# Four of the eight FFN-input passes in fp16 instead of fp32r, in a fused cross-attention and FFN kernel

## The reference

```python
x = x + xattn(layernorm(x), ctx)         # q, k, v, softmax over 256 keys, Wo
x = x + ffn(layernorm(x))
...
def ffn(x):
    h = bitlinear(x, w_fc) + gate * (x @ v.T @ fast_b.T @ u.T)
    r = jnp.maximum(h, 0.0)
    return bitlinear(r * r, w_proj)
def bitlinear(x, w):
    scale = clip(mean(abs(w), axis=1, keepdims=True), 1e-5)
    tern = clip(round(w / scale), -1.0, 1.0)       # -1, 0 or 1
    return x @ (tern * scale).T
```

## Time and profile before

| | us |
|---|---|
| median of the three runs | 782.87 |
| lowest, highest | 781.95, 783.26 |
| profiled execution, span | 782.9 |
| TensorE busy (share) | 769.6 (98%) |
| VectorE busy | 547.3 (70%) |
| ScalarE busy | 368.8 (47%) |
| GpSimd busy | 107.1 (14%) |

### The profile page before, as it was taken

The page is one execution under the profiler, slowest core; times in us unless marked ns, Lnnn a source line. Parts: engine busy times, 40 slices in busy tenths (PEclk is TensorE's granted clock), DMA queues, the critical chain, the costliest instruction groups (busy, mean ns, idle before and its releaser), DMA issues.

```text
span 782.9 us, 10596 instructions
## 1 busy us (share of the span) xinstructions
PE 769.6 (98%) x3767; PEld 639.7 (82%) x3767; DVE 547.3 (70%) x1118; ACT 368.8 (47%) x690; POOL 107.1 (14%) x125
## 2 busy tenths in 40 slices
PE   7999999999999999999999999999999999999997
PEld 4578788888888888888888888888888888888886
DVE  4899776867767687767767786768667686656434
ACT  4899644363434545344533644254442644233332
POOL 3101220200311020110312011210202003000001
PEclk9999999999999999999999999999999999999999
DMA  9644341073214422073214422063212530030101
GB/s 275 245 152 145 54 95 41 1 108 68 81 41 65 66 71 95 1 106 71 80 41 54 69 80 94 2 91 57 109 41 32 80 92 1 1 54 2 53 0 55
DMA packets 180126, 56.20 MB, mean 72 GB/s; under 512 B 167621, under 2 KB 167895, under 8 KB 180073
## 3 DMA queue, kind: packets, MB, share of 16 engines
q1 hardware_dynamic: 149940, 50.79, 26.9%
q10 hardware_dynamic: 30132, 4.73, 3.7%
HBM read 26.92 MB, written 8.39 MB: 45 GB/s over the span
## 4 chain that ended last, share of the span: by engine, by line
PE 95%; SPq 1%; DMA 1%; DVE 1%; issue 0%; ACT 0%; POOL 0%; POOLq 0%; DVEq 0%; ACTq 0%
PE H L1357 30%; PE O L1338 29%; PE G L1220 26%; PE H L1363 4%; PE H L1220 1%; PE H L1204 1%; DMA Wv_s<-in_L_xattn_Wv_dram 1%; PE O L1412 1%; PE G L1304 1%; PE H L1197 1%; PE O L1378 0%; PE G L1248 0%; SPq L518 0%; SPq L556 0%; PE O L1395 0%
## 5 line engine op out<-in xcount | busy, mean ns | idle before, releaser
L1338 PE MATMUL O<-projT,qbuf 128*128 128x512 f32 x992 | 242.1, 390 | 0.0
L1338 PEld LDWEIGHTS O<-projT,qbuf 128*128 128x128 f32 x992 | 185.0, 188 | 38.2
L779 ACT ACTIVATE rbuf<-H,scf 128x512 f32<-128x512 f32 x128 | 87.5, 683 | 125.2 <-DVE qbuf L1116 73.5
L1357 PE MATMUL H<-even_group,fcT 128*128 128x512 f32 x512 | 127.5, 391 | 0.0
L1357 PE MATMUL H<-odd_group,fcT 128*128 128x512 f32 x512 | 127.3, 391 | 0.0
L1112 DVE TENSOR_TENSOR rbuf<-rbuf 128x512 f32<-128x512 f32 x128 | 91.4, 722 | 46.4 <-ACT rbuf L779 46.4
L787 ACT ACTIVATE qbuf<-rbuf 128x512 fp32r<-128x512 f32 x125 | 78.6, 628 | 89.5 <-PE O L1338 62.6
L1116 DVE TENSOR_TENSOR qbuf<-rbuf,qbuf 128x512 fp32r<-128x512 f32 x125 | 85.8, 687 | 37.0 <-ACT qbuf L787 36.2
L1357 PEld LDWEIGHTS H<-odd_group,fcT 128*128 128x128 f32 x512 | 95.3, 188 | 19.3
L1357 PEld LDWEIGHTS H<-even_group,fcT 128*128 128x128 f32 x512 | 95.1, 188 | 19.2
L1220 PE MATMUL G<-Wvo,tT 128*128 128x512 f32 x270 | 64.7, 389 | 0.0
(11 more groups left out here) (194 smaller groups left out, 993.3 us busy)
## 6 DMA issues: line engine op xcount, KB each, us to landing
xb<-in_x_dram SPq DMA_DIRECT2D x8, 1024.0 KB, 5.2
n_blocks<-n_rows SPq DMA_DIRECT2D x112, 64.0 KB, 2.3
ctxb<-in_ctx_dram SPq DMA_DIRECT2D x8, 768.0 KB, 4.4
n_blocks<-ctxb SPq DMA_DIRECT2D x112, 48.0 KB, 2.2
wring<-in_L_ffn_w_fc_dram SPq DMA_DIRECT2D x16, 256.0 KB, 5.8
wring<-in_L_ffn_w_proj_dram SPq DMA_DIRECT2D x16, 256.0 KB, 2.7
out_dram<-x2a SPq DMA_DIRECT2D x8, 512.0 KB, 2.7
x_blocks<-x_rows SPq DMA_DIRECT2D x56, 64.0 KB, 3.5
```

The costliest lines, as they stand in the source:

```text
L779: nc.scalar.activation(rbuf[:, j % 2, :], banks[f"H{j % 2}"][:, :], ACT.Relu, scale=scf[:, j:j + 1]).then_inc(relu_made, 1)
L1338: mm = pe.matmul(banks[f"O{t}"][:, :], qbuf[:, j % 2, h, t * P:(t + 1) * P], projT[:, j, :], start=(j == 0 and h == HI), stop=(j == NFF - ...
L1357: pe.matmul(banks[f"H{j % 2}"][:, :], fcT[:, k, j * P:(j + 1) * P], xnT[:, h, k, :], start=(k == 0 and h == HI), stop=False)
```

## The change

The high half of the FFN input is now an fp16 array of its own (`hi16_of`, laid over a part of the group's array). In `up` four passes multiply it by the ternary weights read as bf16, which is the upper two bytes of each fp32 word (`fc16`, every second 2-byte element); then four passes in fp32r take the low half, which is now the rest over fp16. Before, high and low alternated. `L` keeps fp32r, so GpSimd copies the fp16 halves into fp32r places that are free then (`xhi32`): four new steps `x32:k` in the prologue and in bodies 0 to 6. L waits for all four. In the prologue each of them waits for the last ScalarE copy of x.

```diff
@@ orders of the steps (ACT and DVE of BODY_ORDER; POOL of all three) @@
-        "hi:11 up:12 nc0+ xhi0 up:13 xhi1 xhi2 hi:12 hi:13 up:14 up:15 hi:14 nc1+ nc2+ hi:15 xhi3 nc3+ "
+        "hi:11 up:12 nc0+ xhi0 up:13 xhi1 xhi2 hi:12 hi:13 up:14 up:15 hi:14 xhi3 nc1+ hi:15 nc2+ nc3+ "
-        "residual xs23+ a:0 a:1 a:2 a:3 cs23+ "
+        "residual xs23+ a:0 a:1 a:2 a:3 cs23+ x32:0 x32:1 x32:2 x32:3 "
...
@@ buffers @@
+        hi16_of = [None, under("odd_hi16", [P, KD, TOK], FP16)]
...
+        hi16_of[0] = under("even_hi16", [P, KD, TOK], FP16)
...
+        fc16 = fcT[:, :, :].bitcast(BF16).rearrange("p k (n h) -> p k n h", h=2)[:, :, :, 1]
+
+        def xhi32(g, k):
+
+            return group_of[(g + 1) % 2 if k < 2 else g % 2][:, HI, 2 + k % 2, :]
@@ GpSimd @@
+                    elif st[0] == "x32":
+
+                        k = st[1]
+                        if b < 0:
+                            pool.wait_ge(unit_act, n_act(b, ("x", 3)))
+                            pool.wait_ge(rounded_made, 28)
+                        else:
+                            pool.wait_ge(xhi_made, KD * b + k + 1)
+                        nc.gpsimd.tensor_copy(xhi32(g, k), hi16_of[g % 2][:, k, :]).then_inc(xhi32_made, 1)
@@ ScalarE: x in the prologue, xhi in the bodies @@
-                    nc.scalar.activation(group_of[0][:, HI, :, cols], wide, ACT.Copy).then_inc(unit_act, 1)
+                    nc.scalar.activation(hi16_of[0][:, :, cols], wide, ACT.Copy).then_inc(unit_act, 1)
...
-                        nc.scalar.activation(halves[:, HI, k, :], raw[:, LO, k, :], ACT.Copy).then_inc(xhi_made, 1)
+                        nc.scalar.activation(hi16_of[(b + 1) % 2][:, k, :], raw_of[(b + 1) % 2][:, LO, k, :], ACT.Copy
+                                             ).then_inc(xhi_made, 1)
@@ VectorE: xlo in the bodies (x in the prologue likewise) @@
-                        nc.vector.tensor_tensor(halves[:, LO, k, :], raw[:, LO, k, :], halves[:, HI, k, :],
+                        nc.vector.tensor_tensor(halves[:, LO, k, :], raw[:, LO, k, :], hi16_of[(b + 1) % 2][:, k, :],
                                                 ALU.subtract).then_inc(xlo_made, 1)
@@ TensorE: L @@
+                    highs = [(FB[:, k, :], xhi32(b, k)) for k in range(KD)]
+                    pe.wait_ge(xhi32_made, KD * (b + 1))
                     if b == 0:
                         job_read(pe, JOBS.index(("fb", 0)))
-                        pe.wait_ge(unit_act, n_act(-1, ("x", 3)))
-                        products(bank[:, :], [(FB[:, k, :], xnT[:, HI, k, :]) for k in range(KD)], last=False)
+                        products(bank[:, :], highs, last=False)
                         pe.wait_ge(unit_dve, n_dve(-1, ("x", 3)))
...
                     else:
-                        pe.wait_ge(xhi_made, KD * b)
-                        products(bank[:, :], [(FB[:, k, :], xnT[:, HI, k, :]) for k in range(KD)], last=False)
+                        products(bank[:, :], highs, last=False)
                         pe.wait_ge(xlo_made, KD * b)
@@ TensorE: up @@
                         for k in range(KD):
-                            for h in (HI, LO):
-                                pe.matmul(banks[f"H{j % 2}"][:, :], fcT[:, k, j * P:(j + 1) * P], xnT[:, h, k, :],
-                                          start=(k == 0 and h == HI), stop=False)
+                            pe.matmul(banks[f"H{j % 2}"][:, :], fc16[:, k, j * P:(j + 1) * P], hi16_of[b % 2][:, k, :],
+                                      start=(k == 0), stop=False)
+                        for k in range(KD):
+                            pe.matmul(banks[f"H{j % 2}"][:, :], fcT[:, k, j * P:(j + 1) * P], xnT[:, LO, k, :],
+                                      start=False, stop=False)
```

More of the change, by code:

```diff
@@ L239 @@
     "pool": (
-        "scale:0 tb xs23 scale:1 scale:2 cs23 scale:3 scale:4 scale:5 scale:6 scale:7 B.xs23 a:0 a:1 a:2 a:3 B.cs23 "
+        "scale:0 tb xs23 scale:1 scale:2 cs23 scale:3 scale:4 scale:5 scale:6 scale:7 B.xs23 a:0 a:1 a:2 a:3 x32:0 x32:1 x32:2 x32:3 B.cs23 "
     ).split(),
@@ L366, in mk_xattn_ffn, with under @@
         setup.close()
-        def under(name, shape):
+        def under(name, shape, dt=F32):
             with ExitStack() as below_it:
-                return sb(name, shape, F32, below_it)
+                return sb(name, shape, dt, below_it)
         raw_of = [None, under("odd_halves", [P, 2, KD, TOK])]
+        hi16_of = [None, under("odd_hi16", [P, KD, TOK], FP16)]
         odd = sb("odd_group", [P, 2, KD, TOK], F32R)
@@ L438, in mk_xattn_ffn @@
         xraw_made, xhi_made, xlo_made = sem("xnT_raw_made"), sem("xnT_hi_made"), sem("xnT_lo_made")
+        xhi32_made = sem("xnT_hi_made_for_the_low_rank_passes")
         MOVES = 16 * 16
@@ L809, in steps @@
                         k = int(kind[3])
-                        raw, halves = raw_of[(b + 1) % 2], group_of[(b + 1) % 2]
                         act.wait_ge(xraw_made, KD * b + k + 1)
-                        nc.scalar.activation(halves[:, HI, k, :], raw[:, LO, k, :], ACT.Copy).then_inc(xhi_made, 1)
+                        nc.scalar.activation(hi16_of[(b + 1) % 2][:, k, :], raw_of[(b + 1) % 2][:, LO, k, :], ACT.Copy
+                                             ).then_inc(xhi_made, 1)
                     elif kind == "xmove":
@@ L957, in unit @@
                 if kind == "x":
-                    nc.vector.tensor_tensor(group_of[0][:, LO, :, cols], wide, group_of[0][:, HI, :, cols], ALU.subtract
+                    nc.vector.tensor_tensor(group_of[0][:, LO, :, cols], wide, hi16_of[0][:, :, cols], ALU.subtract
                                             ).then_inc(unit_dve, 1)
```

## The result

| | before | after |
|---|---|---|
| median of 8 runs, us | 782.84 | 786.2 |
| lowest, highest | 781.95, 783.26 | 783.53, 789.52 |
| profiled execution, span | 782.9 | 786.7 |
| TensorE weight loads busy | 639.7 | 588.5 |
| VectorE busy | 547.3 | 557.3 |

After takes 1.0042 times as long as before, interval 1.0023 to 1.0061: 3.4 us slower, where 782.1 us was forecast. A run's time is its span and some 2 us outside it, so the profiled execution of after is the run of 788.88 us, the second slowest of its eight, and that of before, with a span of 782.9 and 1.8 us outside, stands for some 784.7 us and not for the median.

The account below looks back on a forecast made before the run. TensorE's matmul passes times their spacing were taken as the bound. Spacing -5.4, L's wait +3.0, clock +1.6 and bodies 0 gave -0.8 us from 782.9, so 782.1 us; range 779.6 to 785.0, likeliest case's own 780.4 to 783.8.

Parts of the forecast that it names:

- Part 1: TensorE `up` steps: 512 passes going from fp32r to fp16 drop from 226.7 to 216.2 ns, -5.4 us.
- Part 2: `up` steps: 128 changes from fp32r to fp16 and back cost 0, ends 0 and 15.4 us.
- Part 3: Prologue: first L waits for four GpSimd copies of 0.74 us each, +3.0 us, ends 2.1 and 5.1.
- Part 4: Behind the prologue stall: TensorE's clock likelier than not falls to half speed, +1.6 us, ends 0 and 2.7.
- Part 5: Bodies: xhi3 and x32:3 finish before L needs them, cost 0, dear end 7 x 0.2 us.
- Rival C: `up` steps: going back to fp32r costs even behind a long pass; at 0.12 us, 797.5 us; chance 0.06.
- my signs of being wrong: `up` step staying 2.04 us, first fp32r pass after fp16 late, copy over 1 us, or TensorE waiting in bodies.
- Rival B: `up` passes at L1357: type change gives no spacing gain, +4.6 us, 787.5 us; chance 0.12, half a mild form.
- A2: Prologue: the clock holds after the stall, -2.4 us, 780.5 us; chance 0.25.
- D: Prologue: L's wait for the GpSimd copies is covered, -5.4 us, 777.5 us; chance 0.05.
- unseen waits: Bodies: waits that the prediction did not see, no size given; chance 0.05.

Follow-up runs that it names:

- The last two experiments: projT stored as dense fp16, against the whole FFN in 16 bit: 759.1 us; fp16 halves at every second element, against all up passes in fp16: 785.07 us.

## Why the prediction was wrong

| step | predicted, us | found, us |
|---|---|---|
| Part 1, spacing in fp16 | -5.4 | -5.4 by the 216 ns |
| Part 2, changes of type | 0 | +4.5 |
| Part 3, wait of L | +3.0 | +2.2 |
| Part 4, the clock | +1.6 | +1.2 in the mean of the runs, an estimate |
| Part 5, bodies | 0 | 0, no wait |
| outside the span | not seen | +0.3 |
| unassigned | | +0.6 |

**Part 1 was right in its number, and its reason was only half of it.** fp16 passes stand at 216 ns, as 213.3 + 2.9 had it. I put the 13 ns down to fp32r. The last two experiments show 9 to 11 ns also for 16-bit passes whose moving operand is read at every second element, and none for dense ones. fp32r and these have in common that 4 bytes lie between one column's element and the next. Plain f32 at 3.4 ns on top has them too but takes twice as long a column. That this step is what costs the time in fp32r too is argued from them; no run here has fp32r with another step.

**The step that failed is Part 2**, "In the new order it has a pass of 216 ns, so I cost it at 0". I looked for the price at the first fp32r weight load and found it hidden, which is right: the first intervals behind the fp16 group are 448 ns for two. The price lies elsewhere: 3 ns on the last fp32r pass ahead, 12 on the first fp16 one, 5 at the turn back, and 1 to 9 on each of the next six passes. Summed it is 50 ns in dense places and 35 ns over all 128 steps, 4.5 us: five sixths of Part 1. The interval that I used showed 120 ns over eight passes behind an fp16 step; I put all of it to a load with too little cover and so saw no reason for any cost behind a long pass, though the row could not tell one late pass from many slow ones. The trace of before could. Start to start around that step it has 230 ns going in, 67 for the first fp16 pass where the next two have 56, and behind the last one 28 + 318, then 231, 236, 228, 233 and 231 before it is back at 226: the same pattern as in after, pass by pass. About 25 of the 120 ns are those five slow passes, and only the rest is the late load. Rival C had "at 0.03 us, +3", which is 785.9 us, 0.3 us from the median; I gave the whole of C 0.06. Its size came true in the changes of type, but its sign, a late first fp32r pass, did not, and the wait and the clock that stand beside it in the sum were sized too high, so the close number is in part luck. Its high end of 0.12 did not come. Of my signs of being wrong one came, and with this cause: the `up` step of 2.03 us, where 2.00 would have meant a gain.

What makes these passes slow is open. It follows a change of type, not the pace, the lines or the bank; it is paid once a group, whether of four or eight passes (50 ns both times in dense places), and less for single ones in turn (21 ns for each further pair). It is gone where nothing changes (216 ns at all 18 positions). No kernel here separates the weight load's side from the moving operand's.

**Part 3's mechanism was right, its size too large**: a copy took 0.58 us, not 0.74. The cast plus 384 elements at the memset's rate had given 0.61; I chose higher. The Trainium skill, "GPSIMD Engine Reference", section "Elementwise — side-by-side cycle accounting", gave 769 ns for 512 elements in a tight loop; this measured 585 in the prologue, though 618 to 795 in the means of the groups that hold the bodies' copies, so its figure is met only there. From the start of `bvrep`'s passes to L the trace has 2.3 us more than before.

**Part 4 named a fall that can come, and held it for likelier than it was.** The fall right behind the wait is in the trace of the kernel with halves in turn; after's own trace, that of the wait alone and that of fp16 last have the same 2.2 us of wait and no fall behind it. Counting runs with a mean clock of 0.998 or lower: with the 2.2 us wait 4 of 8, 4 of 6, 3 of 4 and 0 of 1; without it, 16 of 47 runs of before and 14 of 50 of the other kernels. So runs with the wait had a fall somewhere in about 6 of 10, the others in 3 of 10; with 19 runs that makes the wait a likely cause, not a certain one. The one behind the wait was 3.4 us long, 1.7 us of loss, as the prediction had it. The mean of the runs is +1.2 because before has falls as well.

**Part 5 was right.** xhi3 and x32:3 are early enough: the copy in body 3 ends at 447.70, L starts at 449.21.

```profile
447.08 0.62 POOL L668 CAST even_group<-even_hi 128x512 fp32r<-128x512 f16 x1 [6.54 <-ACT even_hi L829]
```

VectorE's products take 35 ns more in the mean, and nothing waits for them:

```profile
L1130 DVE TENSOR_TENSOR rbuf<-rbuf 128x512 f32<-128x512 f32 x128 | 95.8, 757 | 46.0 <-ACT rbuf L797 46.0
```

Rival B, no gain in the spacing, forecast 787.5 us, 1.3 us from the median, but by another way: 216 ns stands in the trace of after. Its warning rested on the Trainium skill, "TensorE: Matmul & The Clock Gate", section "Weight-path perf modes — Fast Weight Load (FWL) and DoubleRow", which has the faster 16-bit load win at a small free dimension. At 512 columns 16-bit passes with a dense moving operand are 10.5 ns shorter all the same. That does not go against the section, since the gain is not shown to come from the weights' side: a moving operand with gaps takes it back. A2's holding clock came in half of the runs and D's covered wait in none, but with the 4.5 us of Part 2 lost, a run without a fall is not faster than before either. Of the chances, those for "slower" add up to 0.17 (half of B, C and unseen waits) and not to 0.19.

## What to carry to other kernels

Where matmuls bound a kernel, change the type of whole chains, not of a part of the passes between others: a few dozen ns a change eat the 10 ns a pass that 16 bits give. And give the moving operand its elements side by side: reading bf16 out of fp32 words saves the copy but costs the whole gain when that array moves, and nothing when it is the stationary one. Here the two together made 759.1 us, 3.2% under before, where the change as made lost 0.4%. And read the starts pass by pass around the one place where the old kernel already does what the new one will do: there the price of this change was on record.

## What the runs showed that was not expected

- Six to seven fp32r passes behind a group of 16-bit passes run at 228 to 236 ns instead of 227.
- A 16-bit pass of 512 columns takes 216 ns with a dense moving operand and 224 to 227 ns with one at every second element, the same as fp32r. Bf16 weights at every second element as the stationary operand cost nothing (216 ns).
- The time outside the span is 1.8 us in the kernels without the GpSimd copies in the bodies, before among them, and mostly about 2.1 in those with them (1.9 to 2.2, but 1.8 in one of the 12 runs with copies by token tile). The one with the prologue's copies alone has 1.8. Why is open.
- The clock falls in the early prologue come and go from run to run, in before as in the others, and are up to 6.8 us long: runs of one kernel differ by some 3 us for that alone.
- In three of the twelve traces TensorE still ran at half pace until 20 to 23 us, which cost 2 to 3 us and which the view of the granted clock gives as 1.00.
